# Rebuilding the opening of a graph-attention kernel: bias products on VectorE, scales from sums of squares, and four value tiles before the folding

## The reference

```python
h = relu(layernorm(x))                       # 4096 x 512
q = h @ W_q.T + b_q;  k = h @ W_k.T + b_k;  v = h @ W_v.T + b_v
z = (q @ k.T) / sqrt(512) * adj
z = where(z == 0, -10000, z)
out = x + relu(softmax(z, axis=1) @ v)
```

## Time and profile before

| | us |
|---|---|
| median of 3 runs (1470.32 to 1470.91) | 1470.58 |
| the profiled execution's own time | 1470.61 |
| its span in the trace | 1468.8 |
| PE busy | 1459.6 (99%) |
| DVE busy | 1301.7 (89%) |
| ACT busy | 867.7 (59%) |

### The profile page before, as it was taken

One profiled execution on the slowest core, in us unless ns is written; L12 is line 12 of the kernel. 1 busy time (PEld: TensorE's weight loads), 2 busy tenths in 40 slices (PEclk: granted clock), 3 DMA queues, 4 the chain that ended last, 5 costly groups with the idle time before them and its releaser, 6 DMA issues.

```text
span 1468.8 us, 24830 instructions
## 1 busy us (share of the span) xinstructions
PE 1459.6 (99%) x9510; PEld 935.7 (64%) x9510; DVE 1301.7 (89%) x1597; ACT 867.7 (59%) x1398; POOL 44.7 (3%) x27
## 2 busy tenths in 40 slices
PE   9999999999999999999999999999999999999999
PEld 4466666766666666666666666666666666666555
DVE  7968888899989899999989899989898999988986
ACT  4666665765556656665666555655665566555542
POOL 0000000000000000100010001000000001000100
PEclk9999999999999999999999999999999999999999
DMA  6455535465546665566556664666466645654242
GB/s 208 172 195 176 190 137 216 162 261 215 213 188 234 243 229 191 229 244 220 202 199 251 223 227 192 244 242 217 192 242 244 219 191 211 236 218 177 93 160 99
DMA packets 75190, 301.25 MB, mean 205 GB/s; under 512 B 8512, under 2 KB 8768, under 8 KB 73280
## 3 DMA queue, kind: packets, MB, share of 16 engines
q1 hardware_dynamic: 75072, 299.66, 54.9%
HBM read 260.84 MB, written 38.80 MB: 204 GB/s over the span
## 4 chain that ended last, share of the span: by engine, by line
PE 98%; DVE 1%; DMA 0%; ACT 0%; SPq 0%; issue 0%; POOL 0%; ACTq 0%; DVEq 0%
PE o L651 44%; PE za L593 22%; PE zd L593 11%; PE o L580 6%; PE o L563 6%; PE zb L593 6%; PE o L545 1%; PE zb L651 1%; PE za L662 0%; DMA slots<-in_L_gnn_W_q 0%; PE zb L662 0%; PE zd L680 0%; PE zd L662 0%; POOL floor_b L518 0%; SPq L426 0%
## 5 line engine op out<-in xcount | busy, mean ns | idle before, releaser
L651 PE MATMUL o<-v_buf,p_buf 128*128 128x512 f16 x3072 | 726.5, 376 | 0.8 <-DVE p_buf L1270 0.6
L651 PEld LDWEIGHTS o<-v_buf,p_buf 128*128 128x128 f16 x3072 | 300.4, 98 | 260.8 <-issue 1.5
L593 PE MATMUL za<-h_buf,g_buf 128*128 128x256 f16 x2952 | 402.2, 273 | 0.7 <-ACT um_tmp L845 0.7
L593 PEld LDWEIGHTS za<-h_buf,g_buf 128*128 128x128 f16 x2952 | 287.7, 98 | 138.1 <-ACT mm_tmp L823 2.2
L593 PE MATMUL zd<-h_buf,g_buf 128*128 128x256 f16 x1476 | 201.3, 273 | 0.0
L862 ACT ACTIVATE slots<-slots,log_p 128x1024 f32<-128x1024 f32 x128 | 146.0, 1141 | 51.5 <-DVE slots L1263 51.4
L1270 DVE TENSOR_TENSOR p_buf<-slots,p_buf 128x1024 f16<-128x1024 f32 x128 | 157.4, 1230 | 14.5 <-PE zb L651 13.6
L1263 DVE TENSOR_TENSOR slots<-slots,floor_b 128x1024 f32<-128x1024 f32 x128 | 170.0, 1330 | 0.3 <-POOL floor_b L518 0.3
L1226 DVE TENSOR_TENSOR slots<-um_tmp,dm_tmp 128x512 f32<-128x512 f32 x128 | 89.2, 697 | 78.8 <-ACT dm_tmp L850 78.8
L857 ACT ACTIVATE slots<-za,c_all,kappa 128x256 f32<-128x256 f32 x128 | 72.1, 563 | 142.6 <-PE za L593 141.6
L1238 DVE SCALAR_TENSOR_TENSOR slots<-slots 128x1024 f32<-128x1024 f32 x128 | 156.0, 1218 | 0.2
(11 more groups left out here) (155 smaller groups left out, 1148.3 us busy)
## 6 DMA issues: line engine op xcount, KB each, us to landing
g_buf<-g_dram SPq DMA_DIRECT2D x108, 896.0 KB, 5.2
v_buf<-v_dram SPq DMA_DIRECT2D x128, 512.0 KB, 3.3
adj_own<-in_adj SPq DMA_DIRECT2D x92, 512.0 KB, 6.1
spare<-in_adj SPq DMA_DIRECT2D x36, 512.0 KB, 6.1
g_dram<-g_buf SPq DMA_DIRECT2D x12, 896.0 KB, 4.4
v_dram<-v_buf SPq DMA_DIRECT2D x16, 512.0 KB, 5.3
spare<-in_x SPq DMA_DIRECT2D x15, 512.0 KB, 8.0
h_buf<-h_dram SPq DMA_DIRECT2D x7, 1024.0 KB, 9.3
```

The lines of the kernel that those rows point to most:

```text
L593: mm = pe.matmul(bank[:, 0:QH], g_of(i)[:, a, op, j, :], right[b][j], start=(fresh and j == 0 and m == 0), stop=(j == 1 and m == 2), skip_ ...
L651: mm = pe.matmul(bank, a[:, kt, span], v_buf[:, n % V_BUFS, kt, b, c:d], start=(j == 0 and kt == 0 and m == 0), stop=(j == PAIRS - 1 and k ...
```

## The change

The prologue is rewritten, and the order of the first steps of the loop.

- Loads: W_k, W_q and x come interleaved by pieces (piece e of each), b_q and b_k after the first piece each, laid out by the host so that a partition reads its four values in one run; W_v comes after the second pieces.
- w and u: ACT multiplies the first pieces by their bias column, DVE adds the other three (`add_w`, `add_u`, six instructions over 512 columns); PE sums over the partitions with a ones matrix, one product of 512 columns for w and four of one column for u. The four broadcasts of b_q on DVE, four products for w, four for u and the row's copy and transpositions go.
- Scales: in place of the largest entry, ACT sums squares (`Square` with an accumulated output) of W_v in one instruction of 2048 columns, of M in four of 512 and of u; for W_v a ones product on PE sums over partitions, for M POOL does. ACT takes the square root. `magnitude` loses its first reduction and keeps four links.
- M is computed in the order of the pieces (e outer), with the other work in between.
- `project_v(0)` and `(1)` are in the prologue, between the transpositions, `(2)` and `(3)` at k = 0 and 1; steps k = 2 and 3 have no value product.
- `high_m` and `low_m` are at k = 0 in place of k = 2 and 3. The statistics of the third quad are at k = 1 and 2, with `quad_rstd(2)` at k = 3 in place of k = 2, and ACT's `square_root(2)` stands at the end of k = 2.

The diff, cut to its core:

```diff
-TINY = 1e-30
...
+TINY = 1e-18
...
-HEADROOM = (16.0, 4.0)
+HEADROOM = (1024.0, 256.0)
+U_SHARE = 0.125
...
@@ scheduling helper
+            if k < QUAD:
+                return k + 2 if k < 2 else -1
             return k if k < TILES - 2 else TILES - 2 + k - LATE if k >= LATE else -1
...
@@ sync (DMA queue)
-            sp.dma_start(b_cols[:, 0, :], bq.rearrange("(k p) -> p k", p=P),
-                         allow_slow_non_contiguous=True).then_inc(bq_loaded, 16)
-            def load_wk(e):
+            for e in range(KC):
                 sp.dma_start(wk_raw[:, e, :], wk[e * P:(e + 1) * P, :]).then_inc(wk_loaded[e], 16)
-            def load_first_x(t):
-                sp.dma_start(x_quad[0][:, t, :], x_quads[0][:, t, :]).then_inc(x_first_loaded[t], 16)
-            load_wk(0)
-            load_first_x(0)
-            load_wk(1)
-            sp.dma_start(b_cols[:, 1, :], bk.rearrange("(k p) -> p k", p=P),
-                         allow_slow_non_contiguous=True).then_inc(bk_loaded, 16)
-            load_first_x(1)
-            load_wk(2)
-            load_wk(3)
-            load_first_x(2)
-            load_first_x(3)
-            for e in range(KC):
+                if e == 0:
+                    sp.dma_start(b_cols[:, 0, :], bq).then_inc(bq_loaded, 16)
                 sp.dma_start(wq_raw[:, e, :], wq[e * P:(e + 1) * P, :]).then_inc(wq_loaded[e], 16)
-            sp.dma_start(wv_raw, wv_t.rearrange("(k p) n -> p k n", p=P)).then_inc(wv_loaded, 16)
+                if e == 0:
+                    sp.dma_start(b_cols[:, 1, :], bk).then_inc(bk_loaded, 16)
+                sp.dma_start(x_quad[0][:, e, :], x_quads[0][:, e, :]).then_inc(x_first_loaded[e], 16)
+                if e == 1:
+                    sp.dma_start(wv_raw, wv_t.rearrange("(k p) n -> p k n", p=P)).then_inc(wv_loaded, 16)
             load_x(1)
...
@@ gpsimd
-            for k in range(2):
-                pool.wait_ge(mag_ready, k + 1)
-                nc.gpsimd.partition_all_reduce(mag_all[k][:, :], mag[k][:, :], P, ABSMAX).then_inc(mag_reduced, 1)
+            pool.wait_ge(square_m_ready, KC + 1)
+            nc.gpsimd.partition_all_reduce(square_all[:, :], square[1][:, :], P, TOTAL).then_inc(squares_reduced, 1)
...
@@ tensor
+                if t == 1:
+                    pe.wait_ge(norm_ready, 1)
...
-                pe.wait_ge(wv_lo_ready, KC)
...
+                    if t == 0:
+                        pe.wait_ge(wv_lo_ready, k + 1)
...
-            def product_m(d):
-                for e in range(KC):
-                    if d == 0:
-                        pe.wait_ge(wq_loaded[e], 16)
+            def products_m(e, first, last):
+                pe.wait_ge(wk_loaded[e], 16)
+                pe.wait_ge(wq_loaded[e], 16)
+                for d in range(first, last + 1):
                     mm = pe.matmul(m_bank[d][:, :], wk_raw[:, e, d * P:(d + 1) * P], wq_raw[:, e, :],
                                    start=(e == 0), stop=(e == KC - 1))
-                mm.then_inc(m_ready, 1)
+                    if e == KC - 1:
+                        mm.then_inc(m_ready, 1)
             pe.wait_ge(zeros_ready, 1)
             for _ in range(WARM_UPS):
                 pe.matmul(m_bank[0][:, 0:P], zeros[:, :], zeros[:, :], start=True, stop=True)
-            pe.wait_ge(wide_ready, KC)
-            for e in range(KC):
-                pe.wait_ge(wk_loaded[e], 16)
-                mm = pe.matmul(w_bank[:, :], bq_wide[:, e, :], wk_raw[:, e, :], start=(e == 0), stop=(e == KC - 1))
-            mm.then_inc(w_ready, 1)
-            product_m(0)
+            products_m(0, 0, 3)
+            products_m(1, 0, 3)
+            products_m(2, 0, 1)
+            pe.wait_ge(ones_ready, 1)
+            pe.wait_ge(square_v_ready, 1)
+            pe.matmul(norm_bank, ones[:, :], square[0][:, 0:1], start=True, stop=True).then_inc(square_v_summed, 1)
+            products_m(2, 2, 3)
+            pe.wait_ge(w_part_ready, KC)
+            pe.matmul(w_bank[:, :], ones[:, :], w_part, start=True, stop=True).then_inc(w_ready, 1)
+            products_m(3, 0, 2)
             pe.wait_ge(ident_ready, 1)
             transpose_h(0)
+            products_m(3, 3, 3)
+            pe.wait_ge(u_part_ready, KC)
+            for d in range(KC):
+                mm = pe.matmul(u_bank[:, d:d + 1], u_part[:, d * P:(d + 1) * P], ones[:, 0:1], start=True, stop=True)
+            mm.then_inc(u_ready, 1)
             transpose_h(1)
-            pe.wait_ge(bk_loaded, 16)
-            for e in range(KC):
-                mm = pe.matmul(u_row_bank, b_cols[:, 1, e:e + 1], wq_raw[:, e, :],
-                               start=(e == 0), stop=(e == KC - 1))
-            mm.then_inc(u_row_ready, 1)
+            project_v(0)
             transpose_h(2)
+            project_v(1)
             transpose_h(3)
-            product_m(1)
-            pe.wait_ge(u_row_copied, 1)
-            for d in range(KC):
-                mm = pe.transpose(u_bank[:, d:d + 1], u_row[:, d * P:(d + 1) * P], ident[0:1, 0:1])
-            mm.then_inc(u_ready, 1)
-            product_m(2)
-            product_m(3)
...
@@ scalar
+            def square_m(k):
+                act.wait_ge(m_ready, k + 1)
+                nc.scalar.activation(m_square[:, k, :], m_bank[k][:, :], ACT.Square,
+                                     accum_out=square[1][:, k:k + 1]).then_inc(square_m_ready, 1)
+            act.wait_ge(bq_loaded, 16)
+            act.wait_ge(wk_loaded[0], 16)
+            nc.scalar.activation(w_part, wk_raw[:, 0, :], ACT.Copy, scale=b_cols[:, 0, 0:1]).then_inc(w_part_ready, 1)
+            act.wait_ge(bk_loaded, 16)
+            act.wait_ge(wq_loaded[0], 16)
+            nc.scalar.activation(u_part, wq_raw[:, 0, :], ACT.Copy, scale=b_cols[:, 1, 0:1]).then_inc(u_part_ready, 1)
+            act.wait_ge(wv_loaded, 16)
+            nc.scalar.activation(wv_square, wv_raw.rearrange("p k n -> p (k n)"), ACT.Square,
+                                 accum_out=square[0][:, 0:1]).then_inc(square_v_ready, 1)
+            act.wait_ge(square_v_summed, 1)
+            nc.scalar.activation(top[0][:, :], norm_bank, ACT.Sqrt).then_inc(norm_ready, 1)
+            high_wv(0)
+            high_wv(1)
             square_root(0)
+            high_wv(2)
+            high_wv(3)
             act.wait_ge(w_ready, 1)
             nc.scalar.copy(w_all, w_bank[:, :]).then_inc(w_copied, 1)
             normalise(0)
             normalise(1)
             high_h(0)
+            square_m(0)
+            square_m(1)
             high_h(1)
             normalise(2)
+            keep_h(0)
+            square_m(2)
+            high_h(2)
+            high_v(0)
+            keep_h(1)
             normalise(3)
-            keep_h(0)
-            keep_h(1)
-            high_h(2)
+            square_m(3)
+            act.wait_ge(u_copied, 1)
+            nc.scalar.activation(u_square[:, :], u_cols[:, :], ACT.Square, scale=U_SHARE,
+                                 accum_out=square[1][:, KC:KC + 1]).then_inc(square_m_ready, 1)
+            high_v(1)
             high_h(3)
             keep_h(2)
+            square_root(1)
+            act.wait_ge(square_sum_ready, 1)
+            nc.scalar.activation(top[1][:, :], square_sum[:, :], ACT.Sqrt).then_inc(norm_ready, 1)
             keep_h(3)
-            act.wait_ge(u_row_ready, 1)
-            nc.scalar.copy(u_row, u_row_bank).then_inc(u_row_copied, 1)
-            act.wait_ge(wv_loaded, 16)
-            for k in range(KC):
-                high_wv(k)
-            square_root(1)
             normalise(4)
...
-                between = v_tile(k) < 0
+                between = v_tile(k) < 0 and g >= 1
...
+                if k == 0:
+                    high_m(0)
+                    high_m(1)
                 if g + 1 < QUADS:
                     high_h(k + QUAD)
+                if k == 0:
+                    high_m(2)
+                    high_m(3)
...
-                    for d in range(KC):
-                        high_m(d)
...
@@ vector
-            def largest(dst, src):
-                return v.tensor_reduce(dst, src, AX_X, ALU.max, apply_absolute_value=True)
             def magnitude(k):
-                dve.wait_ge(mag_reduced, k + 1)
-                link(v.tensor_reduce(top[k][:, :], mag_all[k][:, :], AX_X, ALU.max))
...
-            dve.wait_ge(zeros_ready, 1)
-            dve.wait_ge(bq_loaded, 16)
-            for k in range(KC):
-                v.tensor_scalar(bq_wide[:, k, :], zeros[:, :], b_cols[:, 0, k:k + 1], None, ALU.add
-                                ).then_inc(wide_ready, 1)
-            for t in range(QUAD):
-                row_stats(t)
+            def add_w(e):
+                dve.wait_ge(wk_loaded[e], 16)
+                dve.wait_ge(w_part_ready, e)
+                v.scalar_tensor_tensor(out=w_part, in0=wk_raw[:, e, :], scalar=b_cols[:, 0, e:e + 1], in1=w_part,
+                                       op0=ALU.mult, op1=ALU.add).then_inc(w_part_ready, 1)
+            def add_u(e):
```

(89 more changed lines are left out.)

39 lines of the change are left out of this document (23 added, 16 removed).

## The result

| | before | changed |
|---|---|---|
| median us (11 runs each) | 1470.58 | 1474.98 |
| lowest to highest | 1469.85 to 1471.74 | 1473.82 to 1478.48 |
| profiled execution, its span | 1470.61, 1468.8 | 1477.40, 1475.5 |

The ratio is 1.0036, 95% interval [1.0029, 1.0044]: slower by 4.4 us. The time is inside the range that was given, and beyond the 0.2% within which the likeliest case lay. The profiled execution of the changed kernel is one of its longer ones: four of the eleven runs have a mean granted clock of 0.997 and spans of 1475.1 to 1476.3 (this is one of them), the other seven have 0.998 or 0.999 and spans of 1471.5 to 1473.5. So I read from it where the time goes, and take sizes from medians.

A forecast was written before the change was run, and what follows sets the result against it. The prediction measured the change by the first folding's start on PE, with DVE pacing the opening: 14.6 + 30.2 + 3.05 = 47.8, folding at 49.1 against 47.65, so 1470.58 + 1.45 = 1472.0 us; range 1468.3 to 1476.0.

The forecast's parts named there:

- likeliest case: Whole kernel: DVE paces the opening, +1.45 us to 1472.0, within 0.2% of the kernel before; chance 0.52.
- VectorE paces the rebuilt opening: Opening up to the first folding: DVE sets the pace, and nearly 10 us freed on PE all become idle time.
- Its DVE chain starts at 14.6: Opening on DVE: magnitude(0) starts at 14.6, 3.0 us later than the dense stretch began before.
- this bound: Loads: the last x piece lands at 16.4 if the biases' shorter runs save nothing.
- the nearer end: Loads: pieces at 0.68 us each give 13.8 for the last; third pieces of W_k and W_q near 11.
- DVE's work 30.2 and waits 3.05: DVE from magnitude(0) to the third quad's rstd: 30.2 us of work plus 3.05 of waits, ending at 47.8.
- the second rival: First folding: PE's clock is low when it starts, costing 2.6 more, +4.05 us to 1474.6; chance 0.21.
- Forecast walk 1.45: Opening: walking the in-order lists puts the first folding at 49.1 against 47.65, +1.45 us.
- a late load: Loads: named under a missed or underrated wait of over 1.5 us, 1473.6 to 1475; chance 0.13.
- Square without another table load: ACT's squares: expected without extra loads; the rival, Square needing another table, gave about 1474, chance 0.04.
- The reverse side, TensorE as the pace: Opening: PE sets the pace, folding starts at 37.7, 10 us earlier, 1460.6; chance 0.10, mostly for a gain of 3 to 5.

The follow-up runs named there:

- e3: Changed kernel with ScalarE's square_root(2) behind high_h(7) and VectorE's row_stats of tiles 6 and 7 ahead of low_h(2): 1473.00 us.
- e4: Changed kernel with the third quad's statistics taken over 64 of 512 columns, leaving out part of VectorE's work: 1473.24 us.
- e6: Changed kernel with b_q and b_k laid out and loaded as before, in four-byte runs: 1479.04 us (5 runs).
- e7: Changed kernel with W_v loaded behind all pieces and its scale taken late, after VectorE's bias products and first-quad statistics: 1478.64 us (5 runs).
- e1: Changed kernel with useless matmuls filling TensorE's waits at k = 0, 2, 3 and 4: 1473.62 us.
- e2: Changed kernel with project_g(0, 0) ahead of the transposition of tile 8 at k = 4 on TensorE: 1473.59 us.
- e8: Kernel before, with u computed from one piece of W_q in place of four, 2.6 us less on TensorE: 1470.22 us.

## Why the prediction was right or wrong, point by point

- *VectorE paces the rebuilt opening; TensorE's freed 10 us become idle time.* Shown. The waits came where they were named: before `project_v(0)` (forecast 22.7, measured 24.41), before tile 4 (33.9, 35.54), tiles 6 and 7, and the longest before tile 8 (48.65, 51.00). e3 and e4 confirm the pace: the time falls by 2.0 and 1.7 us, of which 1.5 each are seen on VectorE's own list.
- *Its DVE chain starts at 14.6.* Wrong by 1.56. The step that failed is the loads: the third pieces of W_k and W_q were taken to land near 11 and landed at 13.06 and 13.72, W_v near 10 and landed at 12.38. So the tenth product of M ended at 15.65 for 13.96, and ScalarE's squares of W_v at 14.4 for 12.0. 0.68 us a piece is right from the seventh on; the first six took to 9.7, where the sum had 7.0. In the changed kernel the queue moves 320 GB/s on average from 5 to 10 us and 400 from 10 to 15. I had this bound (16.4 for the last x piece, where 13.72 and four more pieces lead) and took the nearer end. e6 moves only the first pieces, by 1.0, and e7 shows that W_v in between isn't the cause. Why the first 10 us are slow stays open. In the eight traces that share the changed kernel's loads and its order up to `magnitude`, DVE starts between 15.53 and 16.26, so this term is 0.9 to 1.7 from run to run, and e6 shows that it passes through whole.
- *DVE's work 30.2 and waits 3.05.* Right in the sum: from `magnitude` to the end of `quad_rstd(2)` 33.1 us in e1, with the clock kept, for 33.25. Two small errors cancel: the waits there are 2.4 (0.32, 1.34 and 0.74 for the forecast 0.35, 1.55 and 0.85, and none for `low_v(2)`), and the work is 0.5 more.
- *The clock.* The mechanism is that of the second rival, with a chance of 0.21. Its size was 2.6 in one product at 49.1; measured are 2.40 in that product, 0.46 in the transposition before it and 0.7 by the first fall, in the profiled run, which is one of the four long ones, and 1.4 over all in the median (e1). Its place was only half foreseen: it already falls right behind the 2.33 us wait before tile 4, at 36, and not in the stretch from 36.9 to 42.2. The Trainium skill (TensorE: Matmul & The Clock Gate, Why this matters for your kernels) has idle gaps between bursts return the array to half clock, and the fall in the 3.36 us wait agrees; the rows of the kernel before have no such wait. The 2.33 us wait settles nothing: the product behind it is slow here and in e6, and not in e2 and e4.
- *Likeliest 1472.0, within 0.2%.* Missed: 1474.98 is 4.4 above. Forecast walk 1.45, late start 1.56 and clock 1.4 make 4.4, though the first two come from single traces and the third from medians. The walk and the late loads take it just past 0.2% (3.1 above with the clock kept, in e1), and the clock puts it well past. I had listed a late load and a low clock as separate cases with separate chances, and priced them together only at the end of the range. That the second rival's 1474.6 lies so near the result is luck: it had no late start in it, and a clock term nearly twice as large as the median's.
- *Square without another table load.* Right: in the opening there is one load at 0.72, and Square, Sqrt and Copy follow without another. The Trainium skill (ScalarE: Activation LUTs, Table sets) says that cheap functions (relu, copy, identity, abs) stand in every set; Square isn't one of these four, and this trace shows it beside Sqrt.
- *The reverse side, TensorE as the pace.* Refuted: M begins 6.5 us earlier and the folding starts 4.25 later, at 51.90. e8 shows for the kernel before as well that 2.6 us less on TensorE give next to nothing.

## What to carry to other kernels

An engine with an unbroken chain in the trace isn't therefore the one whose work is worth cutting: add up the work of the next busiest engine over the same stage, and walk the in-order lists against each other until the moment that the rest hangs on. Here 2.6 us less on the 99% engine gave 0.3 us. Cuts count by stage, and waits that are created on TensorE can cost twice, once as time and once as clock; here useless matmuls in the waits gave 1.4 us back.

## What the runs showed that I had not expected

- The clock fell right behind a wait of 2.33 us (granted 1.00 in 30 to 35, 0.66 in 35 to 40) in the profiled run of the changed kernel, and not behind the same wait of 2.32 us in e2, where the product behind it took 2.75. The same code up to there thus runs at either speed, and the changed kernel's times spread over 4.7 us where the kernel before has 1.9. Even the kernel before is not wholly free of it: two of its 33 runs beside e1 show a clock of 0.999 and 1471.6 us, 1.1 above their median.
- The time outside the span is 1.7 to 2.1 us in all runs with a clock of 1.000 but one, the kernel before among them. In the changed kernel's eleven runs it lies between 1.8 and 3.0 (1474.98 with a span of 1472.3, for one). I have no explanation, and no run separates it.
- The first four instructions of M took 2.11 us when they followed the warm-ups at once, and 3.75 behind a gap of 1.05 us (e6). It is one trace, and the granted clock reads 1.00 in both.
